# Layer 0's five largest values taken over the partitions by a diagonal and a matmul with ones instead of by GpSimd

## What is computed

```python
def act_qdq(x):
    qmax = 2.0 ** (ACT_BITS - 1) - 1.0
    scale = jnp.maximum(jnp.max(jnp.abs(x)) / qmax, 1e-12)
    return jnp.clip(jnp.round(x / scale), -qmax - 1.0, qmax) * scale
...
x = act_qdq(x)                                 # 1: MX
up = act_qdq(x @ lpbq_dequant(w_up).T)         # 4: MU
gate = act_qdq(x @ lpbq_dequant(w_gate).T)     # 2: MG
sig = fixed_qdq_u16(jax.nn.sigmoid(gate))
gate = act_qdq(gate * sig)                     # 3: MZ
o = act_qdq(gate * up)                         # 5: MP
return o @ lpbq_dequant(w_down).T
```

## Time and profile before

| what | value |
|---|---|
| median of 3 runs | 591.76 us (589.72 to 592.52) |
| the profiled execution | 593.56 us, of which span 591.8 us |
| busy, share of the span: PE / DVE / ACT / POOL | 80% / 56% / 43% / 22% |
| mean granted TensorE clock | 0.872 of full speed |
| PARTITION_ALL_REDUCE on POOL | 5 instructions, 350 to 422 ns each |

### The profile page before, as it was taken

One profiled execution on the slowest core, in us unless ns is written; L12 is line 12 of the kernel. 1 busy time (PEld: TensorE's weight loads), 2 busy tenths in 40 slices (PEclk: granted clock), 3 DMA queues, 4 the chain that ended last, 5 costly groups with the idle time before them and its releaser, 6 DMA issues.

```text
span 591.8 us, 8071 instructions
## 1 busy us (share of the span) xinstructions
PE 470.6 (80%) x2478; PEld 306.6 (52%) x2479; DVE 334.1 (56%) x714; ACT 254.8 (43%) x459; POOL 130.0 (22%) x151
## 2 busy tenths in 40 slices
PE   3777739998995000989899999999997359999993
PEld 2566624445442000878556566666665225776672
DVE  1376558252899699434445545555547724555552
ACT  1324234546786484500445554555544223333220
POOL 4134016603000000011565000010001053444221
PEclk9955558998999555999899999999999659999998
DMA  8700000000000001000019800000003321222000
GB/s 254 195 2 1 0 2 1 3 0 0 0 0 1 0 0 43 0 2 1 1 40 387 325 1 1 2 1 1 1 0 105 112 63 53 59 67 60 24 24 0
DMA packets 27287, 27.06 MB, mean 46 GB/s; under 512 B 11631, under 2 KB 23452, under 8 KB 27005
## 3 DMA queue, kind: packets, MB, share of 16 engines
q1 hardware_dynamic: 25053, 21.59, 11.5%
q0 software_dynamic: 2208, 5.14, 3.0%
HBM read 22.48 MB, written 5.15 MB: 47 GB/s over the span
## 4 chain that ended last, share of the span: by engine, by line
PE 69%; DVE 11%; issue 11%; ACT 4%; POOL 1%; DMA 1%; DVEq 1%; SPq 1%; POOLq 0%; ACTq 0%
PE bank L1399 55%; PE bank L1618 6%; PE bank L1446 3%; PE bank L1764 2%; DVE big_g L1130 1%; PE bank L1636 1%; ACT big_u L740 1%; PE bank L1491 1%; DVE amU L1142 1%; PE bank L1515 1%; DVE amZ L1136 1%; DVE big_u L981 1%; ACT yT L740 1%; DMA gates<-in_g_ffn 1%; DVE stat L974 1%
## 5 line engine op out<-in xcount | busy, mean ns | idle before, releaser
L1399 PE MATMUL bank<-yT,ffn_w 128*128 x192 | 86.4, 613 | 3.3 <-ACTq L796 2.7
L1399 PE MATMUL bank<-ffn_w,big_u 128*128 128x256 f32 x192 | 44.0, 391 | 49.1 <-ACT big_u L740 49.0
L740 ACT ACTIVATE big_u<-bank 77x512 f32<-77x512 f32 (+4 forms) x103 | 58.1, 578 | 22.9 <-PE bank L1474 9.6
L1399 PEld LDWEIGHTS bank<-ffn_w,big_u 128*128 128x128 f32 x192 | 37.6, 197 | 55.4 <-ACT big_u L740 49.9
L1399 PEld LDWEIGHTS bank<-yT,ffn_w 128*128 128x128 f32 x192 | 37.5, 197 | 51.0 <-issue 49.8
L1243 DVE TENSOR_REDUCE mx<-bank 128x4 f32<-128x308 f32 x64 | 30.6, 479 | 55.6 <-PE bank L1399 55.6
L896 ACT ACTIVATE big_g<-big_g 128x308 f32<-128x308 f32 x64 | 29.4, 459 | 56.3 <-DVE big_g L1244 56.3
L1399 PE MATMUL bank<-k_blockdiag,big_g 128*128 128x308 f32 x128 | 45.8, 440 | 0.7 <-ACT yT L740 0.7
L1399 PE MATMUL bank<-big_g,yT 128*128 x92 | 44.1, 623 | 0.7 <-issue 0.7
L1399 PE MATMUL bank<-big_u,yT 128*128 x184 | 41.8, 380 | 1.6 <-DVE yT L1362 1.6
L1618 PE MATMUL bank<-ident,big_g 128*77 128x128 f32 x256 | 41.0, 284 | 0.3
(11 more groups left out here) (249 smaller groups left out, 836.3 us busy)
## 6 DMA issues: line engine op xcount, KB each, us to landing
big_g<-in_L_ffn_W SPq DMA_DIRECT2D x1, 4096.0 KB, 16.9
big_u<-in_L_ffn_W SPq DMA_DIRECT2D x1, 4096.0 KB, 26.3
x_rows<-in_x SPq DMA_DIRECT2D x2, 1024.0 KB, 8.2
ffn_w<-in_L_ffn_b SPq DMA_DIRECT2D x1, 2048.0 KB, 24.9
tmp<-bias_by_distance SPq DMA_DIRECT2D x2, 616.0 KB, 4.9
token_rows<-x_rows SPq DMA_DIRECT2D x1, 1032.0 KB, 7.9
tmp<-in_L_ffn_b SPq DMA_DIRECT2D x1, 1024.0 KB, 5.3
token_rows<-x_rows SPq DMA_DIRECT2D x1, 774.0 KB, 9.6
```

What stands on the lines that cost most here:

```text
L740: act.activation(out_, in_, ACT.Copy, **k).then_inc(done, 1)
L1399: return pe.matmul(out_, lhsT=lhsT, rhs=rhs, start=first, stop=last)
```

## The change

The largest value over the partitions no longer comes from POOL. DVE reduces to one value per partition as before, then multiplies the identity by that column, which gives a 128x128 diagonal (`diag`, or `diag_u` for MU). PE multiplies ones (128x128, stationary) by the diagonal, so that each partition of a bank holds all 128 values in its row. DVE reduces that row to its largest. The five `all_max` calls on POOL are gone. In PE's queue the five matmuls stand at fixed places: MX behind the wait for the three copies of the gate's weights, MG between g = 1 and g = 2 of `layer1_operands`, and MZ, MU and MP between the up matmuls and `down(0)`. On DVE, `step_of` for MG moves ahead of the work on `cscale`, `k1T` and `wgn`.

```diff
-            def all_max(n):
-                pool.wait_ge(s.am_sb, n)
-                k = 2 * (n - 1)
-                pool.partition_all_reduce(sc[:, k + 1:k + 2], sc[:, k:k + 1], P,
-                                          bass.bass_isa.ReduceOp.max).then_inc(s.ar_sb, 1)
-
-            all_max(MX)
...
-            all_max(MG)
...
-            all_max(MZ)
-            all_max(MU)
-            all_max(MP)
...
+            def largest(n, of, d):
+                k = 2 * (n - 1)
+                c.link(dve.tensor_reduce(sc[:, k:k + 1], of, AX.X, ALU.max))
+                dve.tensor_scalar(d, ident[:, :], sc[:, k:k + 1], None, ALU.mult).then_inc(s.am_sb, 1)
+
+            def largest_of_all(n, b):
+                k = 2 * (n - 1)
+                dve.wait_ge(s.ar_sb, n)
+                c.link(dve.tensor_reduce(sc[:, k + 1:k + 2], pb[b][:, 0:P], AX.X, ALU.max))
+
...
-            dve.tensor_reduce(sc[:, 0:1], amY[:, :], AX.X, ALU.max).then_inc(s.am_sb, 1)
-
-            dve.wait_ge(s.ar_sb, MX)
+            largest(MX, amY[:, :], diag[:, :])
+            largest_of_all(MX, 3)
...
-            dve.tensor_reduce(sc[:, 4:5], amZ[:, :], AX.X, ALU.max).then_inc(s.am_sb, 1)
-            dve.tensor_reduce(sc[:, 6:7], amU[:, :], AX.X, ALU.max).then_inc(s.am_sb, 1)
-            dve.wait_ge(s.ar_sb, MZ)
+            largest(MZ, amZ[:, :], diag[:, :])
+            largest(MU, amU[:, :], diag_u)
+            largest_of_all(MZ, 6)
...
+            def over_partitions(n, d, b):
+                pe.wait_ge(s.am_sb, n)
+                mm(pb[b][:, 0:P], ones[:, :], d, True, True).then_inc(s.ar_sb, 1)
+
+            over_partitions(MX, diag[:, :], 3)
+
             def layer1_operands():
                 pe.wait_ge(s.gu_sb, FJ + FJ * NQB)
                 pe.wait_ge(s.wq_sb, 3)
                 for g in range(6):
+                    if g == 2:
+                        over_partitions(MG, diag[:, :], 1)
...
+            over_partitions(MZ, diag[:, :], 6)
+            over_partitions(MU, diag_u, 7)
+            over_partitions(MP, diag[:, :], 6)
```

More of the change, by code:

```diff
@@ L347, in flamingo_kernel @@
         sc = sb("scalars", [P, 32])
+        diag = sb("diag", [P, P])
+        diag_u = part(TMP, 3072, [P, P])
         HF = 3 * QB
@@ L1099, in _ @@
             dve.wait_ge(s.dve_step, c.base)
-            dve.tensor_reduce(sc[:, 2:3], amG[:, :], AX.X, ALU.max).then_inc(s.am_sb, 1)
+            largest(MG, amG[:, :], diag[:, :])
+            largest_of_all(MG, 1)
+            step_of(12, sc[:, 3:4], sc[:, 10:11])
+            dve.sem_inc(s.z_done, 2)
+            dve.sem_inc(s.scal_g, 1)
             dve.wait_ge(s.l1_ps, CSC)
@@ L1114, in _ @@
             dve.tensor_scalar(wgn[:, :], wg[:, :], wss[:, 2:3], None, ALU.mult).then_inc(s.wgn_sb, 1)
-            dve.wait_ge(s.ar_sb, MG)
-            step_of(12, sc[:, 3:4], sc[:, 10:11])
-            dve.sem_inc(s.z_done, 2)
-            dve.sem_inc(s.scal_g, 1)
             def half(h):
@@ L1162, in _ @@
             dve.sem_inc(s.scal_z, 1)
-            dve.wait_ge(s.ar_sb, MU)
+            largest_of_all(MU, 7)
             step_of(16, sc[:, 7:8], sc[:, 10:11])
@@ L1179, in _ @@
             dve.wait_ge(s.dve_step, c.base)
-            dve.tensor_reduce(sc[:, 8:9], amP[:, :], AX.X, ALU.max).then_inc(s.am_sb, 1)
-            dve.wait_ge(s.ar_sb, MP)
+            largest(MP, amP[:, :], diag[:, :])
+            largest_of_all(MP, 6)
             step_of(19, sc[:, 9:10], sc[:, 18:19])
```

## The result

The changed kernel took 597.33 us (median of 6 runs, 594.42 to 601.60), the kernel before 591.24 us (6 runs, 587.47 to 592.85): a ratio of 1.0123, 95% interval 1.0074 to 1.0173. That is slower by some 7 us, outside the forecast range. The profiled execution took 596.22 us with a span of 594.3, only 2.5 us more span than the one of before. So two questions stand: what the trace shows, and what the medians hold beyond it.

The account below looks back on a forecast made before the run. On the chain that ended last PE had 69%, DVE 11%, "issue" 11%. Terms 2.28 + 0.67 + 0.72 + 0.92 - 2.63 = +1.96 us took the median from 591.76 to 593.7 us; stated range 590.3 to 596.6.

Parts of the forecast that it names:

- MX's delay: Ahead of the gate matmuls: PE's matmul waits behind ACT's three copies, so the scalings and PE's start come later, +2.28 us.
- MG's: In the transposes of `layer1_operands`: PE stands for 0.42 us and the matmul delays the transposes behind it, +0.67 us.
- MU was hidden: Behind the up matmuls: MU's step comes about 0.9 us later but costs nothing, as ACT needs it only for its second instruction.
- the 7.36 us on the chain: "Issue" wait ahead of POOL's L591 in the down part, taken for a code load; removing it was forecast to gain 2.63 us.
- the size of the hop: The whole way over the partitions by diagonal, matmul and reduction, for one reduction: 1.39 us at the low clock.
- the size of the down part's gain: Between `down(1)` and `down(2)`: without POOL's load, 3.51 us fall to 0.88, -2.63 us.
- the rival that it comes late: At the gate matmuls after MX: a later rise from 1.2 GHz costs +1.5 us, giving 595.2 us; chance 0.1.
- MZ: Behind the up matmuls: `step_of`, with which ACT starts, comes later, +0.72 us.
- MP: Ahead of the down part: 1.39 us against 0.47, with DVE's scaling next and PE idle behind it, +0.92 us.

Follow-up runs that it names:

- after_again: The changed kernel timed a second time with no edit, against the kernel before: 596.56 us, ratio 1.0088.
- the warm pair: The kernel before and the changed kernel, each with five added matmuls in PE's idle time ahead of the attention: 589.15 and 594.43 us.
- load_hidden: The kernel before plus one 8x1 POOL multiplication behind the five reductions, so POOL's code loads earlier: 596.09 us, ratio 1.0051.
- after_warm: The changed kernel plus five matmuls into an unused bank in PE's idle time ahead of the attention: 594.43 us, ratio 1.0054 to the kernel before.
- before_warm: The kernel before plus five matmuls into an unused bank in PE's idle time ahead of the attention: 589.15 us, ratio 0.9972.
- hybrid_warm: hybrid plus the five matmuls ahead of the attention: 585.40 us, ratio 0.9904 to the kernel before.
- load_hidden_later: load_hidden plus six linked, useless DVE multiplications ahead of MP's step: 592.29 us, ratio 1.0013 to the kernel before.
- hybrid: The kernel before with MX by matmul taken early by PE, the other four on POOL, and load_hidden's added instruction: 594.70 us, ratio 1.0004.

## Why the prediction was wrong

The direction and the mechanism of each part were right: the diagonal's matmul at MX started where forecast (behind ACT's third copy), all of MX's delay reached the gate matmuls, MG's stood in PE's transposes, MU was hidden, and the 7.36 us on the chain were worth 2 us and not 7.4. What failed was the size of the hop, which is in three terms, the size of the down part's gain, and the clock, which the sum had at nothing:

- **The sentence on the clock**, in the rival that it comes late: "It would come out in some executions of either kernel alike, so it should hardly move a median." It doesn't come out alike. By their times 7 of the 18 executions of the changed kernel had the long stretch at 1.2 GHz behind the start of the attention (the five of after_again, and 601.28 and 601.60 us of the first six), against 12 of 86 of the kernel before and none of the six that stand beside the first result. A difference as large as 7 of 18 against 12 of 86 comes about one time in fifty by chance. I had looked for a clock effect at the start of the gate matmuls, where it exists too (the 0.43 us in the table, and 1.2 us in the warm pair), and not 200 us later, in code that the change doesn't touch.
- **The size of the hop.** The forecast was 1.39 us at the low clock, the trace has 1.54. From PE's start to the start of its reader it was 0.84 at MP (235.09 to 235.93) and not 0.67: I had worked it out from transposes that follow each other. The diagonal took 0.28 to 0.29 instead of 0.25, the step from it to PE 0.05 instead of 0.1, the reduction 0.29 as forecast. MX, MZ and MP are 0.16, 0.27 and 0.15 larger.
- **The gain of the down part.** PE's waiting went as forecast (the transposes at 263.27 have no idle time), but the low clock at the start of the down matmuls lasted longer, 4.9 us instead of 3.8, and 0.54 of the 2.63 are missing. In load_hidden, where it lasted 3.5 us, the same stretch gave 2.79.

With these two sizes put right, and 0.43 for the gate matmuls' clock, the sum by the trace is +3.5 instead of +1.96. Without the upper group the changed kernel's first executions have a mean of 596.33 us against 590.84 of the kernel before beside them, +5.5; those of after_again 595.73 against 591.73, +4.0 (here the kernel before's upper group is left out too). Weighted by their 4 and 7 executions that is +4.5. That it equals the 4.45 between the traces of after_warm and before_warm is partly luck, since such a pair moves by half a microsecond and more with the clock at the gate matmuls and in the down part. The two long executions of the first six raise their mean to 598.03, by another 1.7. So of the measured 7.2 us in means (598.03 - 590.84) about 2 were forecast, 1.6 were mis-sized, 1.7 are the long stretches, and some 2 are left that no run separates; the clock at the gate matmuls and the scatter of six executions are what is at hand for them. Without the two long executions the mean, 596.33 us, lies just inside the stated range, which ends at 596.6.

That the long stretch is what separates the two groups is shown by two traces of one kernel; that the matmuls ahead of the attention remove it, by after_warm and hybrid_warm (none in 12 and none in 6 executions, against 7 of 18 and 9 of 11 without them). That a change of the program's timing alone can take it away is likely by load_hidden_later, with the reserve of the two chips. Which executions have it I count from times, since only one of each kernel has a trace; the mean clocks of the executions agree with the counts for the changed kernel and load_hidden, and overlap between the groups for hybrid and, in one execution, for the kernel before. Why the changed kernel meets it more often than the kernel before is open. In seven traces the clock fell from 0.75 us ahead of the attention's start to 0.44 behind it, and the three falls more than 0.2 us ahead are the three long stretches. What sets that moment I have not found.

## What to carry to other kernels

When a reduction moves from an idle engine to one with a long queue, its price is where it stands in that queue: the gate matmuls started 3.6 us later with this one matmul behind a wait for copies that it didn't need than with it ahead. Where TensorE's granted clock falls at a change from sparse to dense work, time both kernels with that place held (some matmuls into an unused bank), or a local gain or loss of 2 us disappears behind a change of 7. And a wait on the chain is worth what the engine behind it lost by it (here 2.1 to 2.8 us), not its own length (7.4). A share of the chain is worth less still: 32 us of "issue" here were another engine's idle time.

## What the runs showed of the hardware that I had not expected

- The stretch at 1.2 GHz behind a fall has no one length: 6.8 us in one and 23.9 in another execution of one kernel, at the same code, and 3.4 in hybrid_warm. By the windows PE was busy at every moment of the 23.4 us shown from after_again's, with scores and transposes, and the clock stayed down.
- A delay of 1.94 us on the critical path went with a median 2.5 us lower against the kernel before beside it (on another chip), and with an attention part 7.2 us shorter in the trace.
- The Trainium skill's GPSIMD Engine Reference, section 2.1, has a load of code at about 6 us; here the waits that I take for it were 5.63, 7.36 and 7.70 us, so the page's figure is near the shortest. It also came back each time POOL went from its reduction to other work (7.55 us ahead of L607 and 7.01 ahead of L670 in the kernel before).
- PE's matmul with an isolated 128x128 float32 operand took 0.80 us at 1.2 GHz and 0.49 at 2.4 GHz, two instructions together.
- POOL's wait was 7.7 us long also when nothing else was waiting for it (load_hidden, and 7.58 in load_hidden_later), and behind it the 8x1 multiplication took 0.99 us in the one and 0.29 in the other.
